# A second phase with three rounded matmul pairs and re-ordered engine queues

## The chip, the cores and the metric

The kernel runs on one core of one Trainium2 chip. The metric is the device time of one execution in microseconds. TensorE is PE (its weight loads PEld), VectorE is DVE, ScalarE is ACT, GpSimd is POOL, SyncE is SP.

## The reference

The input is 16 x 512 tokens of width 128 (8192 tokens). Cut to what matters:

```
xn = layernorm(x)
Q  = xn Wq + bq;  s = softmax(Q Q^T / sqrt(128)) Q            # per sequence of 512
logits = xn phi^T + phi_b                                     # 64 experts x 32 slots
D = softmax over a slot axis, C = softmax over the expert axis
X~ = D^T xn ; clip ; layernorm ; tanh ; Y~ = X~ expert_w + expert_b
x  = x + s * silu(C Y~)
xn = layernorm(x)
i, r = sigmoid gates of xn; a = exp(8 r log sigmoid(lam))
h_t = a_t h_(t-1) + sqrt(1 - a_t^2 + 1e-6) (i * xn W_in)      # scan over the sequence
s  = rmsnorm(h) W_out
g  = silu(sigmoid(xr W_r) * (relu(xk W_k)^2 W_v))             # xr, xk: mixes with the token before
out = x + s * g
```

All of it is float32. Products that need more than one rounded pass are made from a high part (rounded to fp32r) and a low part (what the rounding left).

## The kernel before, in words

The first phase (`tensor1`, `scalar1`, ...) goes over 128 units of 128 tokens by 1024 slots, writes the exponentials of the logits to HBM and accumulates X~. A short middle (`tensor1b`, ...) makes the expert outputs and holds them on chip as a high and a low part (`YHI`, `YLO`). The change touches only the second phase, `tensor2`, `scalar2`, `vector2`, `gpsimd2` and `sync2`, lines 1111 to 2347.

The second phase handles NB = 16 batches of 512 tokens. Each batch passes three stages in successive iterations of a software pipeline: the mixture output and the attention (batch i - 1 and i), then layernorm, gates and scan (i - 2), then the state norm, the output gate and the store (i - 3). The functions are the steps. The order in which each engine gets them is written out by hand, one list per engine inside `for i in range(-2, NB)` and then a tail list for the last batches. Engines run their list strictly in order and wait on semaphores; nothing else sets the order.

Per batch the mixture takes 16 chunks. A chunk is turned by four transposes (`exps_turned`, L1219), copied and rounded on ACT (`chunk_high`, L1585), its rest is formed on DVE (`chunk_low`, L1917), and `combine` adds three fp32r matmuls (L1229, L1230, L1232). `ct` has two banks, the chunk copies three. The attention steps are `project`, `values`, `scores`, `probabilities`, `scaled`, `turn`, `turn_high`, `turn_low` and `weigh`.

Seven matmuls per batch are in plain fp32, which the trace shows as two instructions each: `mean` (L1301, x minus its mean, by the matrix `CENTRE`), `variance` (L1309, mean of squares), `state_mean` (L1352), `ffn_k`, `ffn_r`, `ffn_v` and `state_out`.

ACT computes Exp, Ln, Tanh, Square, Copy, Identity and Relu. Its functions come from table sets, one loaded at a time. `log_table` (L1698) loads the set named `natural_log_exp_and_others`, `tanh_table` (L1702) the set named `exp_and_others`. Both are called by hand at places in the list:

```
def log_table(i):
    if i >= 0:
        e.preload_act_table_set("natural_log_exp_and_others")
```

In the loop each is called twice per iteration. The Ln steps are `state_log`, `deviation_log` and `input_log`; the Tanh steps are `ffn_tanh`, `decay_tanh`, `y_tanh`, `input_tanh` and `ffn_r_tanh`. The Tanh of the middle phase (L1041) has no such call in the code ahead of it; the only call before it, at L359, names the set with Ln. POOL multiplies the loaded exponentials by their weights (`weigh_exps`, L146), eight instructions per batch, and does three element-wise steps of a batch (L2275, L2280, L2286).

## Time and profile before

| quantity | value |
|---|---|
| median of 3 runs | 1187.49 us (1187.18 to 1188.07) |
| span of the profiled execution | 1184.2 us |
| PE, DVE, ACT, POOL busy in the span | 97%, 89%, 83%, 81% |
| granted TensorE clock, mean | 0.998 |

The page gives the profiled execution by its span, from its first to its last instruction; a run's time holds 3.3 us more at the median, which lies around the span. A busy time is the union of the engine's records. Records of one engine can overlap, since the next instruction starts before the last has drained, so the distance between two starts is often shorter than a record. The second phase begins near 600 us; its steady part repeats every 35 us.

### The profile page before, as it was taken

Reading aid. Unit: us, or ns where it says so; the run is one execution under the profiler, and the core shown is the slowest. Engines: PE = TensorE matmul, PEld = TensorE weight load, DVE = VectorE, ACT = ScalarE, POOL = GpSimd, SP = SyncE. Lnnn points to the kernel's source line nnn. Section 1 sums busy time; section 2 is a strip of 40 time slices with the busy share of each in tenths; the row PEclk is TensorE's granted clock in tenths of the full one; section 3 lists DMA queues with packets and bytes.
Section 4 is the critical chain, followed back from the end, with each engine's and each line's share of the span. In section 5 each row is a group of like instructions: output and inputs, shape, how many; then the busy total and the mean of one; then the engine's idle time right before and its main releaser. Section 6 shows DMA issues by size and latency. Waiting matters only on the chain. (4 is left out here: it accounts for less than half of the span.)

```text
span 1184.2 us, 17639 instructions
## 1 busy us (share of the span) xinstructions
PE 1144.7 (97%) x5097; PEld 787.9 (67%) x5097; DVE 1050.1 (89%) x1608; ACT 981.7 (83%) x2128; POOL 958.9 (81%) x770
## 2 busy tenths in 40 slices
PE   5999999999999999999989999999999999999996
PEld 3666666565666666666457777777777777777764
DVE  7999999999999999999767888888888888888887
ACT  5877877877766766766668999999999999999998
POOL 3998999898999999999788777878777788877751
PEclk9999999999999999999999999999999999999999
DMA  4445435434424432443754444344444444444420
GB/s 131 152 152 200 141 140 182 153 128 164 155 109 160 155 133 113 161 156 129 225 188 154 131 142 143 119 147 128 142 143 143 131 128 134 141 128 142 142 72 18
DMA packets 125263, 167.36 MB, mean 141 GB/s; under 512 B 7536, under 2 KB 102000, under 8 KB 125040
## 3 DMA queue, kind: packets, MB, share of 16 engines
q1 hardware_dynamic: 123984, 165.71, 41.4%
q8 instruction: 42, 0.69, 0.2%
q10 hardware_dynamic: 1184, 0.53, 0.2%
q14 instruction: 53, 0.43, 0.1%
HBM read 90.71 MB, written 75.50 MB: 140 GB/s over the span
## 5 line engine op out<-in xcount | busy, mean ns | idle before, releaser
L146 POOL TENSOR_TENSOR exp_slots_loaded<-exp_slots_loaded,slot_max 128x1024 f32<-128x1024 f32 x128 | 323.2, 2545 | 6.6 <-DMA exp_slots_loaded<-exp_slots 3.2
L858 POOL TENSOR_TENSOR dd<-ed,rz 128x512 f32<-128x512 f32 x256 | 267.6, 1051 | 24.7 <-ACT rz L688 23.4
L563 PE MATMUL acc<-dd,xns 128*128 128x512 f32 x512 | 261.1, 592 | 0.7 <-POOL dd L858 0.7
L1917 DVE TENSOR_TENSOR clo<-ct,chi 128x512 fp32r<-128x512 f32 x256 | 171.5, 681 | 24.3 <-ACT chi L1585 21.6
L176 POOL TENSOR_TENSOR ch<-exp_slots_loaded 128x512 f32<-128x512 f32 x128 | 165.9, 1296 | 32.0 <-ACT exp_slots_loaded L666 30.9
L795 DVE TENSOR_REDUCE mr<-lg 128x16 fp32r<-128x512 f32 x256 | 168.0, 685 | 19.3 <-PE lg L506 16.9
L657 ACT ACTIVATE ed<-lg 128x512 f32<-128x512 f32 x256 | 145.6, 594 | 40.3 <-PE lg L540 38.4
L666 ACT ACTIVATE exp_slots_loaded<-lg 128x512 f32<-128x512 f32 x256 | 145.5, 594 | 26.4 <-PE lg L549 24.4
L1585 ACT ACTIVATE chi<-ct 128x512 fp32r<-128x512 f32 x256 | 147.7, 597 | 11.8 <-PE ct L1219 8.3
L1219 PE MATMUL ct<-identity,exp_slots_loaded 128*128 128x128 f32 x1024 | 150.9, 273 | 5.6 <-POOL exp_slots_loaded L146 3.1
L811 DVE TENSOR_REDUCE zd<-ed 128x32 f32<-128x1024 f32 x128 | 154.6, 1208 | 1.5 <-ACT ed L657 1.5
L804 DVE TENSOR_REDUCE mr<-lg 128x32 fp32r<-128x1024 f32 x128 | 155.5, 1215 | 0.0
L1219 PEld LDWEIGHTS ct<-identity,exp_slots_loaded 128*128 128x128 f32 x1024 | 124.0, 140 | 35.5 <-POOL exp_slots_loaded L146 8.4
L549 PE MATMUL lg<-shift_experts_to_slots,mt 128*128 128x512 f32 x256 | 144.9, 596 | 0.7 <-ACT ed L657 0.7
L504 PE MATMUL lg<-phi_then_expert_out,xn_transposed 128*128 128x512 f32 x256 | 140.7, 550 | 0.5 <-ACT exp_slots_loaded L666 0.3
L1229 PE MATMUL yac<-chi,phi_then_expert_out 128*128 128x512 f32 x256 | 128.5, 502 | 0.0
L563 PEld LDWEIGHTS acc<-dd,xns 128*128 128x128 f32 x512 | 95.6, 192 | 22.1 <-issue 2.9
L1232 PE MATMUL yac<-clo,phi_then_expert_out 128*128 128x512 f32 x256 | 102.4, 400 | 0.9 <-DVE clo L1917 0.9
L506 PE MATMUL lg<-phi_then_expert_out,xn_transposed 128*128 128x512 f32 x256 | 102.3, 399 | 0.0
L505 PE MATMUL lg<-phi_then_expert_out,xn_transposed 128*128 128x512 f32 x256 | 101.7, 397 | 0.0
L1230 PE MATMUL yac<-chi,phi_then_expert_out 128*128 128x512 f32 x256 | 101.5, 396 | 0.0
L549 PEld LDWEIGHTS lg<-shift_experts_to_slots,mt 128*128 128x128 f32 x256 | 48.2, 188 | 77.4 <-ACT ed L657 62.0
(315 smaller groups left out, 2500.2 us busy)
## 6 DMA issues: line engine op xcount, KB each, us to landing
exp_slots<-exp_slots_loaded SPq DMA_DIRECT2D x128, 512.0 KB, 3.4
exp_slots_loaded<-exp_slots SPq DMA_DIRECT2D x128, 512.0 KB, 3.5
xns<-xn_rows SPq DMA_DIRECT2D x128, 64.0 KB, 1.9
b_xraw<-in_xT SPq DMA_DIRECT2D x16, 256.0 KB, 3.8
out_t<-b_ti SPq DMA_DIRECT2D x15, 256.0 KB, 2.1
expert_w_late<-in_expert_w SPq DMA_DIRECT2D x5, 512.0 KB, 11.1
xn_rows<-slot_sum SPq DMA_DIRECT2D x8, 256.0 KB, 2.5
expert_w_early<-in_expert_w SPq DMA_DIRECT2D x3, 512.0 KB, 5.8
```

Of the source, the lines that this page charges most:

```text
L146: e.tensor_tensor(rows, rows, joined(SM, b)[:, h].unsqueeze(2).broadcast_to([P, TPB, GC * EPC, NP]), ALU.mult).then_inc(s_we)
L176: e.tensor_tensor(ch[v % 2][:, :], ec[v % RE][:, 0:BANK], ec[v % RE][:, BANK:HS], ALU.add).then_inc(s_ch)
L549: e.matmul(lg[v % 2][:, bank(k)], mt[v % 2][:, :], S2M[:, bank(k)], start=False, stop=True, skip_group_check=True).then_inc(s_s2)
L563: e.matmul(acc[k][:, :], xns[v % RX][:, :], dd[v % RX][:, bank(k)], start=tile == 0, stop=tile == NT - 1, skip_group_check=True).then_inc( ...
L657: e.activation(ed[v % RD][:, bank(k)], lg[v % 2][:, bank(k)], ACT.Exp).then_inc(s_ed)
L795: e.tensor_reduce(mr[v % 2][:, k * HN // 2:(k + 1) * HN // 2], lg[v % 2][:, bank(k)].rearrange("q (n p) -> q n p", p=NP), AX_X, ALU.max).t ...
L804: e.tensor_reduce(mr[v % 2][:, HN:G], lg[v % 2][:, :].rearrange("q (n p) -> q p n", p=NP), AX_X, ALU.max).then_inc(s_mx)
L811: e.tensor_reduce(zd[v % 2][:, :], ed[v % RD][:, :].rearrange("q (n p) -> q n p", p=NP), AX_X, ALU.add).then_inc(s_zd)
L858: e.tensor_tensor(dd[v % RX][:, bank(k)].rearrange("q (n p) -> q n p", p=NP), ed[v % RD][:, bank(k)].rearrange("q (n p) -> q n p", p=NP), ...
L1219: done = e.transpose(ct[c % 2][:, rows(k)], ECL[:, g // GC % RL, k, c % GC * P:(c % GC + 1) * P], IDENT[:, :])
L1585: e.activation(chi[g % RC][:, :], ct[c % 2][:, :], ACT.Copy).then_inc(c_h)
L1917: e.tensor_tensor(clo[g % RC][:, :], ct[c % 2][:, :], hi_f32(chi[g % RC][:, :]), ALU.subtract).then_inc(c_l)
```

## The change

`mean`, `variance` and `state_mean` no longer multiply fp32 data. Each of their inputs is rounded to a high part on DVE (`first_high`, `squares_high`, `state_high`), POOL forms the low part (`first_low`, `squares_low`, `state_low`), and PE makes two fp32r matmuls (`two`). The parts are put into the no longer used tiles of `XT` (`tiles_of(i + 1, ...)`). `state_mean` writes to `lp[2]` except for batch 14, and `state_out` then waits for `state_log`. `scaled`, `scaled_r` and `scaled_k` use Copy with a scale column in place of Identity with a scale and a bias column. In the loop, `log_table` and `tanh_table` are called once per iteration each. The lists of all engines are re-ordered, loop and tail; in SP's list one load is moved behind the load of x. The order of ACT is shown whole, since the prediction follows it; those of PE, DVE, POOL and SP are left out. PE's new order for the part that the prediction walks through is: `exps_turned(4)`, `scores(0)`, `scores(1)`, `input_product(i - 3)`, `combine(2)`, `exps_turned(5)`, `combine(3)`, `scores(2)`, `ffn_r(i - 3)`. POOL's new list has the three low parts between its multiplications: `first_low(i)` after multiplication 3, `state_low(i - 1)` after 5, `squares_low(i)` after 6.

```diff
-            CENTRE = WRAW[:, 0, :]
+            CENTRE_R, MEAN_R = XT[:, 0, 0, :], XT[:, 1, 0, :]
+            CENTRE = hi_f32(CENTRE_R)
...
+            def by_tile(T):
+                return T[:, :].rearrange("q (n d) -> q n d", d=TILE)
+
+            def two(e, out, w, i, parts):
+                e.wait_ge(S[parts], 2 * i + 1)
+                e.matmul(out, w, tiles_of(i + 1, 0), start=True, stop=False)
+                e.wait_ge(S[parts], 2 * i + 2)
+                return e.matmul(out, w, tiles_of(i + 1, 1), start=False, stop=True)
 
 
             LAST = NB - 1
...
 
                 def mean(i):
                     if within(i):
-                        e.wait_ge(S["res"], i + 1)
                         if i:
                             e.wait_ge(S["f1"], i)
                         else:
-                            e.wait_ge(s_zero, 2)
-                        e.matmul(lp[0][:, :], CENTRE, B[f"x1{i % 2}"][:, :], start=True, stop=True).then_inc(S["mn"])
+                            e.wait_ge(s_zero, 3)
+                        two(e, lp[0][:, :], CENTRE_R, i, "x1_parts").then_inc(S["mn"])
 
                 def variance(i):
                     if within(i):
-                        e.wait_ge(S["sq"], i + 1)
                         if i:
                             e.wait_ge(S["ix"], i)
-                            e.wait_ge(S["hl"], i)
-                        e.matmul(lp[1][:, :], MEAN[:, :], B["ty"][:, :], start=True, stop=True).then_inc(S["vr"])
+                        two(e, lp[1][:, :], MEAN_R, i, "sq_parts").then_inc(S["vr"])
 
                 def decay_gate(i):
                     if within(i):
...
-                        e.matmul(lp[1][:, :], MEAN[:, :], B["a2"][:, :], start=True, stop=True).then_inc(S["hm"])
+                        if i == LAST - 1:
+                            e.wait_ge(S["ix"], i + 1)
+                        else:
+                            e.wait_ge(S["kr"], i + 1)
+                        two(e, state_bank(i)[:, :], MEAN_R, i, "hq_parts").then_inc(S["hm"])
 
                 def state_out(i):
                     if within(i):
-                        e.wait_ge(S["hh"], i + 1)
-                        e.wait_ge(S["kr"], i + 1)
+                        e.wait_ge(S["hl"], i + 1)
                         if i == LAST - 1:
                             e.wait_ge(S["ix"], nth(1))
                         e.matmul(lp[2][:, :], WRAW[:, W_OUT, :], B["hh"][:, :], start=True, stop=True).then_inc(S["po"])
...
-                        e.activation(B[f"e{r}"][:, :], B[f"e{r}"][:, :], ACT.Identity, bias=one(EPS, 3),
+                        e.activation(B[f"e{r}"][:, :], B[f"e{r}"][:, :], ACT.Copy,
                                      scale=one(nmx, 4 * r + 3)).then_inc(A["p"])
 
...
-                        e.activation(B["aa"][:, :], lp[1][:, :], ACT.Ln, bias=one(EPS, 1)).then_inc(S["hl"])
+                        e.activation(B["aa"][:, :], state_bank(i)[:, :], ACT.Ln, bias=one(EPS, 1)).then_inc(S["hl"])
 
                 def state_inverse(i):
...
@@ -1769,145 +1781,145 @@
                 for i in range(-2, NB):
                     chunk_high(i - 1, 4)
+                    input_log(i - 3)
+                    input_root(i - 3)
                     next_factors(i)
                     probabilities(i - 1, 0)
                     chunk_high(i - 1, 5)
+                    probabilities(i - 1, 1)
+                    scaled(i - 1, 0)
                     ffn_r_tanh(i - 3)
-                    probabilities(i - 1, 1)
                     chunk_high(i - 1, 6)
-                    scaled(i - 1, 0)
-                    state_squares(i - 3)
-                    scaled(i - 1, 1)
                     probabilities(i - 1, 2)
                     chunk_high(i - 1, 7)
+                    state_squares(i - 3)
+                    log_table(i - 1)
+                    scaled(i - 1, 1)
+                    chunk_high(i - 1, 8)
                     scaled(i - 1, 2)
-                    chunk_high(i - 1, 8)
-                    ffn_tanh(i - 3)
-                    log_table(i - 1)
-                    state_log(i - 3)
+                    squares(i - 2)
                     chunk_high(i - 1, 9)
                     probabilities(i - 1, 3)
                     chunk_high(i - 1, 10)
                     scaled(i - 1, 3)
-                    squares(i - 2)
-                    state_inverse(i - 3)
+                    state_log(i - 3)
                     chunk_high(i - 1, 11)
                     turn_high(i - 1, 0)
                     chunk_high(i - 1, 12)
+                    state_inverse(i - 3)
                     deviation_log(i - 2)
-                    tanh_table(i - 1)
                     deviation_inverse(i - 2)
+                    ffn_tanh(i - 3)
                     turn_high(i - 1, 1)
                     chunk_high(i - 1, 13)
+                    scaled_k(i - 2)
+                    scaled_r(i - 2)
                     chunk_high(i - 1, 14)
-                    scaled_k(i - 2)
                     turn_high(i - 1, 2)
-                    scaled_r(i - 2)
+                    decay_tanh(i - 2)
+                    tanh_table(i - 1)
                     chunk_high(i - 1, 15)
+                    turn_high(i - 1, 3)
+                    decay(i - 2)
                     chunk_high(i, 0)
-                    decay_tanh(i - 2)
-                    decay(i - 2)
-                    turn_high(i - 1, 3)
+                    y_tanh(i - 1)
                     decay_squares(i - 2)
+                    attended(i - 1)
                     chunk_high(i, 1)
-                    y_tanh(i - 1)
-                    log_table(i - 1)
-                    attended(i - 1)
-                    input_log(i - 2)
-                    tanh_table(i - 1)
+                    ffn_k_relu(i - 2)
                     query(i)
                     chunk_high(i, 2)
                     chunk_high(i, 3)
+                    value_high(i)
+                    ffn_k_squares(i - 2)
                     input_tanh(i - 2)
-                    ffn_k_relu(i - 2)
-                    value_high(i)
-                    input_root(i - 2)
-                    ffn_k_squares(i - 2)
             
 
+                tanh_table(LAST)
                 chunk_high(LAST, 4)
+                input_log(LAST - 2)
                 probabilities(LAST, 0)
                 chunk_high(LAST, 5)
+                input_root(LAST - 2)
+                scaled(LAST, 0)
+                probabilities(LAST, 1)
+                probabilities(LAST, 2)
                 ffn_r_tanh(LAST - 2)
-                probabilities(LAST, 1)
                 chunk_high(LAST, 6)
-                scaled(LAST, 0)
-                state_squares(LAST - 2)
                 scaled(LAST, 1)
-                probabilities(LAST, 2)
                 chunk_high(LAST, 7)
                 scaled(LAST, 2)
+                ffn_tanh(LAST - 2)
+                state_squares(LAST - 2)
                 chunk_high(LAST, 8)
-                ffn_tanh(LAST - 2)
-                log_table(LAST)
+                probabilities(LAST, 3)
+                chunk_high(LAST, 9)
+                squares(LAST - 1)
+                scaled(LAST, 3)
+                chunk_high(LAST, 10)
                 state_log(LAST - 2)
-                chunk_high(LAST, 9)
-                probabilities(LAST, 3)
-                chunk_high(LAST, 10)
-                scaled(LAST, 3)
-                squares(LAST - 1)
-                state_inverse(LAST - 2)
                 chunk_high(LAST, 11)
                 turn_high(LAST, 0)
+                state_inverse(LAST - 2)
                 chunk_high(LAST, 12)
+                chunk_high(LAST, 13)
                 deviation_log(LAST - 1)
-                tanh_table(LAST)
                 deviation_inverse(LAST - 1)
+                log_table(LAST)
                 turn_high(LAST, 1)
-                chunk_high(LAST, 13)
-                chunk_high(LAST, 14)
+                log_table(LAST)
                 scaled_k(LAST - 1)
                 turn_high(LAST, 2)
-                scaled_r(LAST - 1)
+                chunk_high(LAST, 14)
                 chunk_high(LAST, 15)
                 decay_tanh(LAST - 1)
+                turn_high(LAST, 3)
                 decay(LAST - 1)
-                turn_high(LAST, 3)
+                y_tanh(LAST)
+                scaled_r(LAST - 1)
+                log_table(LAST)
                 decay_squares(LAST - 1)
-                y_tanh(LAST)
-                log_table(LAST)
-                ffn_k_relu(LAST - 1)
+                input_tanh(LAST - 1)
                 last_squares(0)
+                last_squares(1)
                 input_log(LAST - 1)
                 last_deviation_log(0)
-                last_squares(1)
                 last_deviation_inverse(0)
+                last_deviation_log(1)
+                ffn_k_relu(LAST - 1)
                 input_root(LAST - 1)
-                last_deviation_log(1)
                 last_deviation_inverse(1)
-                tanh_table(LAST)
-                input_tanh(LAST - 1)
+                ffn_r_tanh(LAST - 1)
+                ffn_k_squares(LAST - 1)
                 last_decay_tanh(0)
+                log_table(LAST)
+                last_decay(0)
+                state_squares(LAST - 1)
+                last_decay_squares(0)
+                ffn_tanh(LAST - 1)
                 last_input_tanh(0)
-                ffn_k_squares(LAST - 1)
-                last_decay(0)
                 last_decay_tanh(1)
-                ffn_r_tanh(LAST - 1)
-                last_ffn_r_tanh(0)
+                last_input_tanh(1)
                 last_decay(1)
-                last_decay_squares(0)
-                last_decay_squares(1)
-                last_input_tanh(1)
-                state_squares(LAST - 1)
-                log_table(LAST)
                 last_input_log(0)
                 state_log(LAST - 1)
+                last_decay_squares(1)
+                last_input_root(0)
+                last_ffn_r_tanh(0)
+                state_inverse(LAST - 1)
                 last_input_log(1)
-                last_input_root(0)
-                tanh_table(LAST)
                 last_input_root(1)
-                state_inverse(LAST - 1)
+                last_ffn_tanh(0)
+                last_state_squares(0)
+                last_state_log(0)
                 last_ffn_r_tanh(1)
-                ffn_tanh(LAST - 1)
-                last_state_squares(0)
-                last_ffn_tanh(0)
+                last_state_inverse(0)
+                last_state_squares(1)
                 last_ffn_tanh(1)
-                log_table(LAST)
-                last_state_squares(1)
-                last_state_log(0)
-                last_state_inverse(0)
                 last_state_log(1)
                 last_state_inverse(1)
+                tanh_table(LAST)
+                tanh_table(LAST)
 
             def vector2(e):
...
+
+                def constants(i):
+                    if i == 0:
+                        e.wait_ge(S["q_p"], 1)
+                        e.tensor_tensor(CENTRE_R, IDENT[:, :], MEAN[:, :], ALU.subtract).then_inc(s_zero)
+                        e.tensor_copy(MEAN_R, MEAN[:, :]).then_inc(s_zero)
+
+                def first_high(i):
+                    if within(i):
+                        e.wait_ge(S["res"], i + 1)
+                        e.wait_ge(S["q_p"], i + 2)
+                        e.tensor_copy(tiles_of(i + 1, 0), by_tile(B[f"x1{i % 2}"])).then_inc(S["x1_parts"])
+
+                def squares_high(i):
+                    if within(i):
+                        e.wait_ge(S["sq"], i + 1)
+                        e.tensor_copy(tiles_of(i + 1, 0), by_tile(B["ty"])).then_inc(S["sq_parts"])
+
+                def state_high(i):
+                    if within(i):
+                        e.wait_ge(S["hq"], i + 1)
+                        e.tensor_copy(tiles_of(i + 1, 0), by_tile(B["a2"])).then_inc(S["hq_parts"])
 
                 def normalise(i):
                     if within(i):
```

## Rows read from the trace of the kernel before

**Rows 1.** The page: busy tenths of the span in 40 slices, PE and its granted clock.

```profile
PE   5999999999999999999989999999999999999996
...
PEclk9999999999999999999999999999999999999999
```

**Rows 2.** Stretches of 35 us in the steady part: busy us of PE, PEld, DVE, ACT, POOL; clock.

```profile
892.00:927.00 35.00, 35.00 (x184) 26.77 (x183) 30.12 (x52) 34.16 (x60) 27.50 (x16) 1.00 0.43 138
962.01:997.00 34.99, 34.99 (x184) 26.74 (x183) 30.06 (x52) 34.13 (x59) 27.45 (x16) 1.00 0.43 136
```

**Rows 3.** PE in order of time: start us, us, instruction, count.

```profile
964.03 0.60 PE L1219 MATMUL ct<-identity,exp_slots_loaded 128*128 128x128 f32 x4
964.46 1.02 PE L1301 MATMUL lp<-b_x,weights 128*128 128x512 f32 x2
965.32 1.02 PE L1360 MATMUL lp<-b_hh,weights 128*128 128x512 f32 x2
...
982.29 0.39 PE L1235 MATMUL at<-xn_transposed,weights_high 128*128 128x512 f32 x1
982.52 0.40 PE L1236 MATMUL at<-xn_transposed,weights_high 128*128 128x512 f32 x1
982.76 0.39 PE L1237 MATMUL at<-xn_transposed,weights_low 128*128 128x512 f32 x1
982.99 0.40 PE L1229 MATMUL yac<-chi,phi_then_expert_out 128*128 128x512 f32 x1
```

**Rows 4.** Groups of the second phase: count, busy us, mean ns of one, idle before.

```profile
L1569 ACT ACTIVATE b_e<-b_e,epsilons,nmx 128x512 f32<-128x512 f32 x64 | 51.7, 811 | 0.5 <-DVE nmx L1938 0.5
L1670 ACT ACTIVATE b_a<-b_a,epsilons 128x512 f32<-128x512 f32 x15 | 10.7, 713 | 0.0
L1974 DVE CAST r_xh<-xn 128x512 fp32r<-128x512 f32 x15 | 6.3, 418 | 0.0
L2280 POOL TENSOR_TENSOR r_xl<-xn,r_xh 128x512 fp32r<-128x512 f32 x15 | 19.3, 1290 | 60.8 <-DVE r_xh L1974 60.8
```

**Rows 5.** ACT in order of time, in a steady batch.

```profile
979.28 0.60 ACT L1577 ACTIVATE b_ty<-yac 128x512 f32<-128x512 f32 x1
979.90 1.28 ACT L1698 ACT_TABLE_LOAD   x1
981.19 0.60 ACT L1564 ACTIVATE b_st<-at 128x512 f32<-128x512 f32 x1
981.69 0.71 ACT L1670 ACTIVATE b_a<-b_a,epsilons 128x512 f32<-128x512 f32 x1
982.42 1.28 ACT L1702 ACT_TABLE_LOAD   x1
```

**Rows 6.** ACT in order of time, in the first batch, where no Ln runs yet.

```profile
633.90 1.28 ACT L1698 ACT_TABLE_LOAD   x1
635.20 0.60 ACT L1564 ACTIVATE b_st<-at 128x512 f32<-128x512 f32 x1
635.82 1.28 ACT L1702 ACT_TABLE_LOAD   x1
```

**Rows 7.** Table loads, whole span, by line; count and ns (minimum, median, maximum), first and last start.

```profile
L1698 ACT ACT_TABLE_LOAD  x34: 1283/1283/1283, 619.5 to 1176.4; - x34
L1702 ACT ACT_TABLE_LOAD  x33: 1283/1283/1283, 624.8 to 1172.4; - x33
L1041 ACT ACT_TABLE_LOAD  x1: 1283/1283/1283, 591.9 to 591.9; - x1
```

**Rows 8.** Waits of POOL between 752 and 1032 us: total, times, longest.

```profile
POOL r_xl L2280 <- DVE r_xh L1974: 31.0, 8, 3.9
POOL b_ty L2286 <- DVE b_ty L1953: 19.4, 8, 2.4
POOL r_ql L2275 <- DVE r_qh L1924: 9.1, 8, 1.1
```

**Rows 9.** The tail list, stretch as in rows 2.

```profile
1127.93:1184.20 56.27, 45.02 (x198) 30.35 (x196) 45.00 (x85) 47.75 (x88) 15.68 (x10) 0.96 0.12 38
```

**Rows 10.** ACT's last instruction.

```profile
1180.03 0.42 ACT L1768 ACTIVATE b_e<-b_e 128x256 f32<-128x256 f32 x1
```

More of the change, by code:

```diff
@@ L1439, in tensor2 @@
+                    weigh(i - 2, 3)
                     exps_turned(i - 1, 1)
-                    combine(i - 2, 14)
-                    combine(i - 2, 15)
-                    weigh(i - 2, 2)
-                    weigh(i - 2, 3)
+                    ffn_k(i - 3)
+                    project(i - 1)
                     exps_turned(i - 1, 2)
-                    input_gate(i - 3)
-                    input_product(i - 3)
-                    project(i - 1)
                     combine(i - 1, 0)
@@ L1625, in scaled_r @@
                             e.wait_ge(S["f2"], i)
-                        e.activation(B["xr"][:, :], x_in, ACT.Identity, bias=one(EPS, 3), scale=one(VEC, V_MUR)).then_inc(S["mr"])
+                        e.activation(B["xr"][:, :], x_in, ACT.Copy, scale=one(VEC, V_MUR)).then_inc(S["mr"])
                 def scaled_k(i):
@@ L1632, in scaled_k @@
                             e.wait_ge(S["pk"], i)
-                        e.activation(B["xk"][:, :], x_in, ACT.Identity, bias=one(EPS, 3), scale=one(VEC, V_MUK)).then_inc(S["mk"])
+                        e.activation(B["xk"][:, :], x_in, ACT.Copy, scale=one(VEC, V_MUK)).then_inc(S["mk"])
                 def input_tanh(i):
```

222 lines of the change are left out of this document (125 added, 97 removed), and 2 rows, old and new, of the table S.

## The prediction, made before the changed kernel ran

> **What bounds the kernel now.** I read the page's slices first: PE is busy in nine tenths or more of nearly every slice, at the full granted clock [rows 1]. A high share is an average, so I looked at the steady part of the second phase in stretches of its own period, 35.0 us: there PE has no gap at all, ACT is covered for 34.1, DVE for 30.1 and POOL for 27.5 [rows 2]. PE's records overlap, so I checked by starts that this is real work. Rounded matmuls start 0.23 to 0.24 us apart, a plain fp32 one takes 0.86 us to the next start, four transposes 0.43 [rows 3]. A batch has 48 + 12 + 12 + 3 + 9 = 84 rounded matmuls (combine, scores, weigh, project, three gates), 7 plain ones and 21 sets of four transposes: 84 x 0.233 + 7 x 0.86 + 21 x 0.435 = 34.7, which is the period within 1%. So PE sets the period, and ACT is right behind it. ACT's 0.87 us of gaps, with 0.1 of lost overlap at each of some five gaps (a 0.60 record lets the next start 0.50 later [rows 5]), leaves about 33.7 us of work per batch. DVE has 5 us to spare and POOL 7.5.
>
> The end is another matter. The tail list lasts 56.3 us, and ACT is covered for 47.75 of them, PE for 45.0 [rows 9]. ACT's last instruction ends at 1180.45 [rows 10], 3.75 before the end. ACT leads the tail.
>
> **The change, part by part.**
>
> *PE.* Three plain matmuls of 0.86 become pairs of 0.47: 3 x 0.39 = 1.17 us less per batch, 33.8 in place of 35.0. The old time is on the path.
>
> *DVE.* Three casts of 0.42 each [rows 4], +1.3: 31.4. *POOL.* Three subtractions of 1.29, +3.9: 31.35. Both are covered by the period as long as their waits shrink (a rival, below). Of the new waits, PE's on a low part has nearly all of PE's queue behind it; the lists put other PE work between the step that makes the input and the pair, so I take these waits at zero, with 1 us per batch as the other end. The changed bank of `state_mean`, the move of SP's load and the setup on DVE I cost at nothing: one instruction, or work in the spare time of [rows 2].
>
> *ACT, Copy for Identity.* An SBUF operation with two column operands takes 0.811, with one 0.713 [rows 4]: 0.1 x 6 = 0.6 less per batch.
>
> *ACT, the table loads.* The calls are half as many, but the needs are not. In the new loop list the order is: `input_log` (Ln), `ffn_r_tanh` (Tanh), the call of the Ln set, `state_log` and `deviation_log` (Ln), `ffn_tanh`, `decay_tanh` (Tanh), the call of the Tanh set, `y_tanh`, `input_tanh` (Tanh), and around again to `input_log`. Ln and Tanh alternate twice per batch as before, and the calls no longer stand where the sets change: `input_log` runs with the Tanh set, `ffn_tanh` with the Ln set. The trace shows what then happens: the Tanh at L1041 comes with the Ln set loaded and no call ahead of it, and there is a load on its own line [rows 7]. So loads are placed where they are missing. It also shows that a called load is executed though nothing needs it: in the first batch both are, with only a copy between [rows 6], and the 34 + 33 loads are exactly the calls that the lists make.
>
> Which set a placed load takes for an Ln isn't shown. The code names the set that has Exp too, by hand and before its first Ln, which would be needless if it came by itself; so I take a set with Ln alone, and the Exp behind it needs another load. In the loop the count is the same either way, as the way back comes at `input_root` or at `ffn_r_tanh`. Going down the list: `input_log`, `input_root`, the call of the Ln set, `ffn_tanh`, and the call of the Tanh set, which is loaded already. Five per iteration, four before, from i = 3 on (13 iterations); iterations 1 and 2 have two and three. In the tail I count 26 ahead of the last `last_state_inverse`, where there were 7: it alternates at `input_log`, `state_log`, `deviation_log` of batch 14, at each of `last_input_log` and `last_state_log`, each time there and back.
>
> One load costs 1.29 to the next start, and the instruction ahead of it loses its overlap (0.62 in place of 0.50 to the next start [rows 5]): 1.41.
>
> The Trainium skill, ScalarE: Activation LUTs (What ACT_TABLE_LOAD costs), puts a switch at 2.66 us, 1.283 for the load and 1.38 for a drain. The load agrees to the nanosecond; the drain is not there, since the next instruction starts 1.29 after [rows 5]. By the page's figure the 19 further loads of the tail alone would be 51 us, an estimate, and the kernel would come out near 1245. I go by the row. The same page (Table sets) says that a compiler pass puts a load before every activation that needs one; L1041 agrees.
>
> **The sum.** Steady part: ACT 33.7 - 0.6 + 1.4 = 34.5 us of work, PE 33.8. Neither fits the other: at the head of the loop ACT now has load, Ln, load, Exp, `next_factors` and `probabilities(0)` between two chunks. From the start of `chunk_high(4)` to the end of `probabilities(0)` that is 0.5 + 1.4 + 0.7 + 1.4 + 0.5 + 0.3 + 0.7 = 5.5 us. PE has for it two `scores`, a product, two `combine` (5 x 0.70) and one set of transposes (0.44), 3.9 us, and then `scores(2)` waits for that probability: 1.5 us idle. With 0.4 more near `ffn_tanh`, where Exp, Ln, Exp, load and Tanh stand between two chunks (estimated, since PE can have three chunks ready): 33.8 + 1.5 + 0.4 = 35.7. The ends are 34.5 (all hidden) and 37 (both stalls in full, and waits on the low parts). So 13 x 0.7 = +9. The first iterations have PE's saving only in part: -1.
>
> Tail: work 47.75 + 19 x 1.41 + 1.25 (`input_log` and `input_root` of batch 13 come in from the loop) - 0.6 = 75.2; of the 4.8 us of gaps I keep 2 (ends 1 and 6); and 3.75 behind ACT: 81, where 56.3 was: +24.5.
>
> In all 1184.2 + 9 - 1 + 24.5 = 1217 by the span; runs lie 3.3 above it: 1220. With the ends of the steady part (-6.5 to +26) and of the gaps the likeliest case has 1204 to 1240. A difference under 0.2% can't be told from none.
>
> **The rivals.**
>
> *The repeated call costs nothing.* The compiler could drop a load of the set that is there already. The executed calls of [rows 6] were needless but did change the set, so they don't rule it out. Then 80 loads in place of 98: four per iteration, ACT at 33.1, period about 35.0 with the stall at the loop's head half closed, 22 in the tail less the idle kept: 1187.5 + 0 - 1 + 21 = 1207.
>
> *A placed load for Ln takes the set with Exp too.* Six fewer in the tail, 8.5 us: 1211. For it: a pass that looks ahead would. Against it: the name in the code.
>
> *POOL becomes the bound.* It waits 59.5 us in 8 batches for DVE, 7.4 per batch [rows 8]. 31.35 + 7.4 = 38.8, over the 35.7, if the waits keep their length; it decides from 4.4 us per batch of waits. +3.1 x 13 = +40: 1260. Against it: these waits are slack of a loop that PE paces, and the new list puts the subtractions between multiplications.
>
> *The relief of PE wins (other side).* Both of the first two rivals hold, the tail has 18 loads, 11 more than before, and its gaps take 4: +15.5 - 4 + 0.7 = +12. The new order hides the blocks so that PE stays the bound at 33.9: 13 x -1.1 = -14, and -1 at the start: 1184. The point from which it decides is a period below about 34.1. That the change does as it is called, two loads per batch in place of four and a tail with as few, would give 1187.5 - 15 x 1.17 = 1170; the order of Ln and Tanh in the list rules it out, unless one set held both, and then nothing would have been loaded in between before.
>
> **How the numbers follow.** Forecast 0.52, dropped repeats 0.15, other set 0.15, POOL 0.08, relief of PE 0.08, as it is called 0.02. Slower over 0.2% is the first four, 0.90; of the other 0.10 I give 0.07 to faster and 0.03 to the 0.2% around no change (1184 is near its edge). The range leaves out POOL as the bound and the lowest of the faster cases: 1197 to 1241.
>
> **What would show it.** Plain matmuls at the three lines gone, pairs 0.23 apart. Table loads on lines of Ln, Exp and Tanh steps: 98 in all in the second phase, 28 in the tail; 80 or 92 would be the rivals. ACT covered more than PE in a steady batch, and PE with a gap ahead of the third `scores`, released by ACT. A period of 35.7; 33.9 would show me wrong on the coupling, 38 would be POOL. A tail of 80 us led by ACT. I am wrong altogether if the loads are 30 to 40 in number.

## The result, and the profile after

The changed kernel takes 1296.46 us (median of 4 runs, 1295.71 to 1296.63), where the kernel before took 1187.51 on the same chip: 1.0917 times as long [1.0902, 1.0933]. The direction was forecast; the size (1220, at most 1241) was not. In the profiled execution the span is 1294.8 us, 110.6 more than before.

To see where they are, cut the span at the scan of a batch, an instruction that both kernels run once per batch. Thirteen periods, from the scan of the first batch to that of the fourteenth, last 1224.37 - 678.56 = 545.8 us, 41.7 to 42.5 each and 41.9 at the median; before it was 1130.58 - 675.89 = 454.7, or 35.0 each. So the start holds +2.7, the steady part +91.1, and what follows that scan +16.8 (70.4 for 53.6).

The stretches, columns as in [rows 2]: length, busy us of PE, PEld, DVE, ACT, POOL, clock, DMA share, GB/s. First two steady periods and the end of the kernel after:

```profile
847.01:889.12 42.11, 35.72 (x185) 26.38 (x183) 37.15 (x55) 35.31 (x61) 32.06 (x18) 1.00 0.35 113
930.86:973.07 42.21, 35.67 (x185) 26.40 (x184) 37.22 (x55) 35.31 (x61) 32.06 (x18) 1.00 0.34 113
1224.37:1294.80 70.43, 46.32 (x183) 33.34 (x181) 42.92 (x78) 65.83 (x97) 19.49 (x12) 0.82 0.07 23
```

and the end of the kernel before, cut at the same scan (the list of [rows 9] begins a little earlier):

```profile
1130.58:1184.20 53.62, 42.37 (x184) 28.44 (x182) 42.47 (x79) 45.38 (x83) 15.12 (x9) 0.96 0.12 39
```

The reader is to see two things. In the steady part no engine is covered for the whole period any more: the fullest is DVE with 37.2 of 42.2, and PE has 6.5 us of gaps where it had none. So the engines now wait for each other in turn. And ACT and POOL stand near their forecast (35.3 for 34.5, 32.06 for 31.35), while DVE stands at 37.2 where I had 31.4: its instructions take 5.8 us more than their durations before add up to.

Which of them, the groups of DVE in the second phase of the kernel after tell (line, op, tiles, shapes, count | busy us, mean ns | idle before):

```profile
L2054 DVE TENSOR_TENSOR_SCAN b_hh<-b_aa,vectors,b_ti 128x512 f32<-128x512 f32 x15 | 50.6, 3372 | 0.0
L2074 DVE TENSOR_TENSOR b_ti<-b_aa,b_x 128x512 f32<-128x512 f32 x15 | 37.4, 2490 | 0.5
L2029 DVE TENSOR_SCALAR b_a<-b_a 128x512 f32<-128x512 f32 x15 | 21.1, 1403 | 0.3 <-ACT b_a L1631 0.3
L1989 DVE CAST xn_transposed<-b_ty 128x512 fp32r<-128x512 f32 x15 | 19.8, 1317 | 0.0
L1984 DVE CAST xn_transposed<-b_x 128x512 fp32r<-128x512 f32 x15 | 9.3, 622 | 0.0
L1994 DVE CAST xn_transposed<-b_a 128x512 fp32r<-128x512 f32 x15 | 6.2, 412 | 0.0
```

The kernel before, the same three steps in the same view:

```profile
L2020 DVE TENSOR_TENSOR_SCAN b_hh<-b_aa,vectors,b_ti 128x512 f32<-128x512 f32 x15 | 22.6, 1505 | 0.0
L2040 DVE TENSOR_TENSOR b_ti<-b_aa,b_x 128x512 f32<-128x512 f32 x15 | 10.4, 692 | 0.5
L1995 DVE TENSOR_SCALAR b_a<-b_a 128x512 f32<-128x512 f32 x15 | 6.2, 411 | 0.0
```

The same instruction with the same operands takes 3.37 us in place of 1.50 (the scan), 2.49 in place of 0.69 (`output`), 1.40 in place of 0.41 (`one_minus`). These three alone are 1.87 + 1.80 + 0.99 = 4.7 us per batch, and the cast of the squares adds 0.9. What stands beside the scan and `output` is POOL's multiplication of the exponentials; beside `one_minus` it is another POOL instruction, the product at L2341. The timelines of DVE and POOL (start us, us, instruction, count, [idle before <-releaser]) around one of each, kernel after:

```profile
930.13 0.69 DVE L2046 SCALAR_TENSOR_TENSOR b_ti<-b_ti,b_a 128x512 f32<-128x512 f32 x1
930.86 3.52 DVE L2054 TENSOR_TENSOR_SCAN b_hh<-b_aa,vectors,b_ti 128x512 f32<-128x512 f32 x1
...
930.90 5.63 POOL L146 TENSOR_TENSOR exp_slots_loaded<-exp_slots_loaded,slot_max 128x1024 f32<-128x1024 f32 x2 [2.02 <-DVE b_ti L2046]
...
949.72 2.77 DVE L2074 TENSOR_TENSOR b_ti<-b_aa,b_x 128x512 f32<-128x512 f32 x1
...
949.16 5.57 POOL L146 TENSOR_TENSOR exp_slots_loaded<-exp_slots_loaded,slot_max 128x1024 f32<-128x1024 f32 x2
...
959.75 1.50 DVE L2029 TENSOR_SCALAR b_a<-b_a 128x512 f32<-128x512 f32 x1
...
959.63 1.33 POOL L2341 TENSOR_TENSOR b_ty<-b_ty,b_st 128x512 f32<-128x512 f32 x1
```

and around the scan of the kernel before:

```profile
990.67 1.37 DVE L2020 TENSOR_TENSOR_SCAN b_hh<-b_aa,vectors,b_ti 128x512 f32<-128x512 f32 x1
...
990.06 0.89 POOL L130 TENSOR_TENSOR slot_joined<-slot_sum 128x128 f32<-128x128 f32 x1
990.92 8.01 POOL L146 TENSOR_TENSOR exp_slots_loaded<-exp_slots_loaded,slot_max 128x1024 f32<-128x1024 f32 x3
```

Before, POOL was still at a small step when the scan began, and its multiplication came 0.25 us later. After, POOL has been idle for 2.02 us and is released by the very instruction (L2046, `scan_input`) that also feeds the scan; both start within 0.04 us, and the scan takes 2.1 us longer, about one multiplication. `output` begins 0.56 behind the start of a multiplication and takes 2.1 longer too. `one_minus` begins 0.12 behind POOL's product and takes 1.1 longer, so about 1 us of the 5.8 is not the multiplications'.

Who pays for it shows in the waits of ACT over six steady batches of the kernel after (engine, line, waited for: us in total, times, longest), with PE's behind them:

```profile
ACT b_aa L1619 <- DVE b_ti L2074: 12.9, 6, 2.1
ACT b_a L1692 <- DVE b_hh L2054: 11.9, 6, 2.0
ACT chi L1597 <- PE ct L1232: 11.4, 18, 1.7
...
PE yac L1245 <- DVE clo L1929: 12.3, 12, 1.5
PE at L1278 <- ACT b_e L1561: 9.4, 6, 1.6
```

ACT's two longest waits are for exactly these two instructions: `decay_tanh` needs `output`, `state_squares` needs the scan, 4.1 us per batch together. The chunks behind them on ACT come late, and DVE's low parts, and PE. No wait in the lists of PE, DVE and ACT for these six batches ends on POOL: nobody waits for what POOL makes.

The second suspect, the loads, came as forecast. In order of time on ACT, kernel after:

```profile
964.88 0.60 ACT L1597 ACTIVATE chi<-ct 128x512 fp32r<-128x512 f32 x1
965.49 1.28 ACT L1682 ACT_TABLE_LOAD   x1
966.79 0.72 ACT L1682 ACTIVATE b_a<-b_a,epsilons 128x512 f32<-128x512 f32 x1
967.53 1.28 ACT L1687 ACT_TABLE_LOAD   x1
968.82 0.63 ACT L1687 ACTIVATE b_a<-b_a 128x512 f32<-128x512 f32 x1
```

and in the groups of the whole span:

```profile
L1710 ACT ACT_TABLE_LOAD x19 | 24.4, 1283 | 0.3
L1714 ACT ACT_TABLE_LOAD x17 | 21.8, 1283 | 0.3
L1682 ACT ACT_TABLE_LOAD x15 | 19.2, 1283 | 0.3
L1687 ACT ACT_TABLE_LOAD x14 | 18.0, 1283 | 0.2
L1677 ACT ACT_TABLE_LOAD x14 | 18.0, 1283 | 0.3
```

With 18 more on fourteen lines of Ln, Exp and Tanh steps that is 97 in the second phase (67 before, [rows 7]), five in each steady batch. The Ln at L1682 got a set without Exp, and the Exp at L1687 another load. L1710 and L1714 are the calls: all 19 of the Ln set, and 17 of the 18 of the Tanh set. Repeated calls are executed (L1710 at 1243.41 and, with one copy between, at 1245.32; L1714 in every batch). Of the last two calls in the list, with nothing between them, only one has a record; no run tells why.

### The profile page after: what moved, and what is told of

Same layout as the page of the kernel before. It is cut to its first block, busy times and chain, and to the rows that moved or that the text cites. A ratio compares the mean times of both kernels' runs of the same rounds, so it can differ in the third digit from the quotient of the medians.

```text
span 1294.8 us, 17761 instructions
## 1 busy us (share of the span) xinstructions
PE 1159.8 (90%) x5097; PEld 788.4 (61%) x5097; DVE 1150.5 (89%) x1654; ACT 1017.9 (79%) x2158; POOL 1028.3 (79%) x815
## 4 chain that ended last, share of the span: by engine, by line
DVE 19%; ACT 17%; PE 10%; issue 8%; ACTq 0%; DVEq 0%
DVE clo L1929 4%; DVE b_hh L2054 4%; PE ct L1232 3%; ACT chi L1597 3%; DVE b_ti L2074 3%; PE yac L1245 2%; ACT L1710 2%; ACT L1682 1%; DVE b_a L2029 1%; DVE xn_transposed L1989 1%; DVE b_f L2040 1%; ACT L1677 1%; PE yac L1242 1%; PE yac L1243 1%; ACT b_e L1581 1%
## 5 line engine op out<-in xcount | busy, mean ns | idle before, releaser
L146 POOL TENSOR_TENSOR exp_slots_loaded<-exp_slots_loaded,slot_max 128x1024 f32<-128x1024 f32 x128 | 332.6, 2610 | 66.5 <-DMA exp_slots_loaded<-exp_slots 32.6
L176 POOL TENSOR_TENSOR ch<-exp_slots_loaded 128x512 f32<-128x512 f32 x128 | 165.7, 1295 | 31.4 <-ACT exp_slots_loaded L666 30.3
L795 DVE TENSOR_REDUCE mr<-lg 128x16 fp32r<-128x512 f32 x256 | 168.0, 685 | 18.9 <-PE lg L506 16.5
L1597 ACT ACTIVATE chi<-ct 128x512 fp32r<-128x512 f32 x256 | 152.1, 595 | 35.7 <-PE ct L1232 34.5
L1245 PE MATMUL yac<-clo,phi_then_expert_out 128*128 128x512 f32 x256 | 105.2, 411 | 26.6 <-DVE clo L1929 26.6
L1242 PE MATMUL yac<-chi,phi_then_expert_out 128*128 128x512 f32 x256 | 115.4, 451 | 0.1
L1243 PE MATMUL yac<-chi,phi_then_expert_out 128*128 128x512 f32 x256 | 101.4, 396 | 0.0
```

Of the source, the lines that this page charges most:

```text
L146: e.tensor_tensor(rows, rows, joined(SM, b)[:, h].unsqueeze(2).broadcast_to([P, TPB, GC * EPC, NP]), ALU.mult).then_inc(s_we)
L176: e.tensor_tensor(ch[v % 2][:, :], ec[v % RE][:, 0:BANK], ec[v % RE][:, BANK:HS], ALU.add).then_inc(s_ch)
L795: e.tensor_reduce(mr[v % 2][:, k * HN // 2:(k + 1) * HN // 2], lg[v % 2][:, bank(k)].rearrange("q (n p) -> q n p", p=NP), AX_X, ALU.max).t ...
L1597: e.activation(chi[g % RC][:, :], ct[c % 2][:, :], ACT.Copy).then_inc(c_h)
```

## The experiments

Theory A, held: DVE's instructions are held back by POOL's multiplications, which the new lists put in front of them. Theory B: it is the five loads per batch that stretch the period, by more than I had, and DVE's long records are a by-product. Theory C: POOL has too much work with the three low parts, or PE waits for them.

**e1: the loads taken away.** `Ln` becomes `Square`, so the logarithms are left out, and no call is made; the trace then has no load in the second phase.

```diff
-  e.activation(..., ACT.Ln, ...)
+  e.activation(..., ACT.Square, ...)
-  e.preload_act_table_set(...)      # log_table, tanh_table
+  pass
```

> The changed kernel with no table loads in the second phase: the three Ln steps compute Square (same operands, so the state norm, the deviation and the input factor are wrong) and both calls are left out. Theory A (the DVE instructions held behind POOL pace the loop, 41.9 us): ACT has 7 us less per batch but the scan, the output step and the casts stay long; period 38 to 41, median 1240 to 1280. Theory B (the five loads pace it): period 34 to 35.5, median 1170 to 1190.

Measured: 1221.30 us, 1.0295 [1.0265, 1.0325]. The period is 38.1, the scan still takes 3366 ns on average. The end, from the scan of the fourteenth batch on, is 47.2 us, where it was 70.4. So taking the loads away gives 75 us: 3.8 per batch (about 50), 23 in the end, the rest at the start. The period is in the range that A expected, the time below it, since the end gave back so much. Not all of the 3.8 is the loads' own time: `output` falls from 2490 to 1058 ns as POOL's work now meets DVE's elsewhere, while the cast of the squares rises from 1317 to 1841. Without a single load the new kernel is still 2.95% slower than before: B can't be all.

**e2: the low parts taken away.** The second matmul of each pair takes whatever lies in the low tiles, and PE doesn't wait for it, so the low parts are left out; POOL has 3.9 us less per batch.

```diff
-  first_low(i) ... state_low(i - 1) ... squares_low(i)    # POOL
-  e.wait_ge(S[parts], 2 * i + 2)                          # PE
```

> The changed kernel without POOL's three low parts; both rounded matmuls are still made, the second from what lies in the low tiles (its sum is wrong). The casts stay. Theory A: POOL has 3.9 us less per batch, but its multiplications still start just ahead of the scan and the output step, so the scan stays near 3.5 and the period falls by 1 to 3 us: 1250 to 1280. Theory C (PE's waits on low parts pace it): period 36 or less, under 1215.

Measured: 1313.30 us, 1.107 [1.103, 1.1111]. Less work, and slower than the change by 17 us. That ends C, and missed what I expected. The groups of DVE in e2 show what came with it:

```profile
L2053 DVE TENSOR_TENSOR_SCAN b_hh<-b_aa,vectors,b_ti 128x512 f32<-128x512 f32 x15 | 50.6, 3371 | 0.0
L2073 DVE TENSOR_TENSOR b_ti<-b_aa,b_x 128x512 f32<-128x512 f32 x14 | 36.6, 2617 | 0.5
L1993 DVE CAST xn_transposed<-b_a 128x512 fp32r<-128x512 f32 x15 | 31.7, 2115 | 0.2 <-ACT b_a L1691 0.2
```

The multiplications begin at other moments, and the cast of the state's squares, 412 ns in the change, is held for 1.7 us as well.

**e3: POOL released by the scan itself**, not by its input, so that the scan is first.

```diff
-  e.wait_ge(S["gt"], i - 1)     # weigh_exps, k == 4
+  e.wait_ge(S["hh"], i - 1)
```

> The changed kernel, in which POOL's multiplication 4 waits for the scan instead of for the scan's input. Theory A: the scan falls from 3.5 to about 1.4 us, ACT's 2.0 us wait for it is gone; POOL starts 1.4 later. Period down by 1 to 2.5 us, 1260 to 1280. If the long scan were not caused by POOL's start: no shorter scan, same or slower than 1296.

Measured: 1292.09 us, 1.0892 [1.086, 1.0923]. Groups of DVE in e3:

```profile
L2074 DVE TENSOR_TENSOR b_ti<-b_aa,b_x 128x512 f32<-128x512 f32 x15 | 37.4, 2493 | 0.5
L1994 DVE CAST xn_transposed<-b_a 128x512 fp32r<-128x512 f32 x15 | 35.5, 2365 | 0.0
L1989 DVE CAST xn_transposed<-b_ty 128x512 fp32r<-128x512 f32 x15 | 27.6, 1843 | 0.0
L2054 DVE TENSOR_TENSOR_SCAN b_hh<-b_aa,vectors,b_ti 128x512 f32<-128x512 f32 x15 | 19.4, 1293 | 0.0
```

The order of release does decide who is held: the scan is at 1293 ns now. But the 2.1 us moved on to the next cast (412 to 2365), and the time gained is 4 us of 109, where 16 or more were expected; the intervals of e3 and of the change overlap. One hold taken away isn't a hold less.

**e4: the new orders without the split.** The three plain matmuls stay as before, no casts, no low parts; lists, calls and `Copy` as in the change.

```diff
-  two(e, lp[0][:, :], CENTRE_R, i, "x1_parts")
+  e.matmul(lp[0][:, :], CENTRE, B[f"x1{i % 2}"][:, :], start=True, stop=True)
```

> The new orders, Copy and calls with the three matmuls in plain fp32 as before: no casts, no low parts. PE has 1.17 us more per batch, DVE 3 casts less, POOL 3 subtractions less. If the orders and loads are what costs: period 37.5 to 41, 1235 to 1285. If the split into parts is what costs: near 35 to 36, 1190 to 1215.

Measured: 1300.26 us, 1.096 [1.0929, 1.0992]: the whole loss, and 4 us more, is there without the split, and more than I expected of the orders. The scan (3372 ns) and `output` (2488) are as long as in the change. The lists and the calls lose the time. If the split itself gives anything back, it is those 4 us, and the intervals of e4 and of the change touch.

**e5 and e6: the multiplications halved**, with the loads of the change (e5) and without any (e6). Only the first two of four blocks of `weigh_exps` are multiplied.

```diff
-  e.tensor_tensor(rows, rows, ..., ALU.mult)
+  e.tensor_tensor(rows[:, 0:2], rows[:, 0:2], ..., ALU.mult)
```

> The changed kernel in which POOL's multiplications of exponentials do two of their four tiles (half the elements; the rest of the weighting is left out). Loads as in the changed kernel. Theory A (DVE held behind POOL's instructions): the longest hold falls from 2.1 us to 1 us, the scan to 2 to 2.5 us, DVE's busy time by 3 us; period from 41.9 to 38.5 to 40. Theory B (the loads alone): DVE's times fall but the period stays over 41.

> Both at once: half of the multiplications and no table loads (Ln steps as Square). If loads and holds explain the excess between them, the period comes to PE's own 33.8 to 34.8, from 38.1 without loads alone; median 1150 to 1175. If a third cause is there (waits between PE and the new orders), it stays over 36.

Measured: e5 1243.68 us, 1.0484 [1.0463, 1.0505], with the scan at 2353 ns and `output` at 1534; e6 1177.55 us, 0.9927 [0.9907, 0.9947]. The periods of the four, from scan to scan, at the median:

```
                        five loads   no loads
multiplications whole      41.9        38.1
multiplications half       38.2        35.1
```

A stretch of one period of e6, columns as above:

```profile
847.00:882.12 35.12, 34.57 (x184) 26.68 (x183) 32.44 (x55) 28.80 (x56) 22.93 (x18) 1.00 0.42 134
```

The period of e5 is just under what A expected, that of e6 and its time are just over their ranges. Both causes are real, of equal size, and nearly add up: the loads give 3.8 or 3.1, half of the multiplications 3.7 or 3.0. With both gone PE is covered again for 34.57 of 35.12 us. Half sized multiplications also take 9 us per batch of work off POOL, so e5 alone would not tell a hold from a full POOL; e2 does that, where POOL had 3.9 us less and nothing was gained, and so does the list of waits above, in which nobody waits for POOL.

**e7: a load only where the set changes**, and for every Ln the set that has Exp too.

```diff
-  e.preload_act_table_set(...)        # log_table, tanh_table
+  with_log()    # ahead of each Ln: loads its set unless it is there
+  with_tanh()   # ahead of each Tanh, the same
```

> The changed kernel in its own order, but each load placed where the needed set changes, for Ln always the set that has Exp too: 4 per batch in place of 5, and 17 or so in the tail in place of 26. Outputs complete. By loads at 0.76 us of period each (3.8 us for five): 41.1 in the steady part, -11; tail about 9 loads less, -10; 1273 to 1280.

Measured: 1279.96 us, 1.079 [1.0768, 1.0812], with 67 loads again in the second phase, as many as before, and as expected. The period is 41.3, the end 62.9. So calls in the right places would have saved 16.5 us of 109: 0.7 per batch on average (the fifth load) and 7.5 in the end. By e1 the other four loads are worth 3.8 - 0.7 = 3.1 per batch in this order, where [rows 2] had four inside PE's time.

**e8: the split in the old order.** The lists and calls of the kernel before; the mean and the mean of the state's squares in two passes, their casts and low parts set into the old lists; `state_mean` stands two steps later in PE's.

```diff
     value_low(i)            # DVE
+    first_high(i - 1)
...
     chunk_low(i, 6)
+    state_high(i - 2)
```

> The kernel before with its own orders and loads, and two of the three matmuls (mean and state mean) in two rounded passes, the casts and low parts put into the old lists. PE has 0.78 us less per batch. If PE still paces it: 15 x 0.78 = 12 less, 1175. If the two casts (0.8) and two low parts (2.6) are held or hold the scan: between 1180 and 1205.

Measured: 1225.19 us, 1.0319 [1.0302, 1.0336], period 37.4, over both ranges expected. Here the scan is as before (1504), but the new cast `first_high` (L1981) takes 1955 ns, and ACT's exponentials wait 1.6 us per batch for a maximum behind it on DVE (`b_e` L1558 for `nmx` L1942: 8.0, 5 times). So the split meets holds in the old list too. How much of the 2.4 us of period they make isn't shown.

**e9: the hold by itself.** Thirteen equal instructions on DVE, 128 x 512; behind the fifth, POOL is released for four multiplications of 128 x 1024; once for each of four forms.

```
DVE: out = a + b      (both SBUF)      POOL: big = big * factor, four
DVE: out = ps + b     (PSUM and SBUF)        times, from DVE's fifth
DVE: cast a to the rounded type
DVE: scan over a, b
```

> A kernel by itself, none of the reference's work: DVE runs 13 times each of four forms on 128x512 (sum of two SBUF tiles, sum of a PSUM and an SBUF tile, cast of an SBUF tile to fp32r, scan of two SBUF tiles), and POOL four multiplications of 128x1024 beside the last eight. Theory A (held by the operands): the first, third and fourth form get longer by up to a POOL instruction (2.1 us) or make POOL longer; the PSUM form stays at 0.68. If any DVE instruction is slowed by POOL, the PSUM form grows too; if none is, the long ones in the changed kernel have another cause.

Each form's line (count: minimum/median/maximum ns, first and last start), then the groups with their means:

```profile
L72 DVE TENSOR_TENSOR from_two_sbuf<-left,right x13: 679/685/2828, 6.8 to 22.7; 128x512 f32<-128x512 f32 x13
L74 DVE TENSOR_TENSOR from_psum_and_sbuf<-ps,right x13: 677/677/680, 23.3 to 30.4; 128x512 f32<-128x512 f32 x13
L76 DVE CAST from_cast<-left x13: 414/421/2564, 36.1 to 48.7; 128x512 fp32r<-128x512 f32 x13
L77 DVE TENSOR_TENSOR_SCAN from_scan<-left,right x13: 1252/1252/3293, 49.0 to 71.3; 128x512 f32<-128x512 f32 x13
L95 POOL TENSOR_TENSOR multiplied<-multiplied,factor x16: 2337/2550/3229, 10.1 to 64.8; 128x1024 f32<-128x1024 f32 x16
...
L77 DVE TENSOR_TENSOR_SCAN from_scan<-left,right 128x512 f32<-128x512 f32 x13 | 23.5, 1881 | 0.0
L72 DVE TENSOR_TENSOR from_two_sbuf<-left,right 128x512 f32<-128x512 f32 x13 | 16.5, 1342 | 0.0
L76 DVE CAST from_cast<-left 128x512 fp32r<-128x512 f32 x13 | 13.0, 1077 | 4.9 <-POOL multiplied L95 4.9
L74 DVE TENSOR_TENSOR from_psum_and_sbuf<-ps,right 128x512 f32<-128x512 f32 x13 | 7.9, 677 | 0.0
```

Mean less median, times 13, over four multiplications: an addition of two SBUF operands loses 13 x 0.657 / 4 = 2.1 us to each multiplication, the cast 2.1, the scan 2.0, and the addition with one PSUM operand nothing (its longest is 680 ns). That is nearly the multiplication's own 2.34. And it falls on one instruction for each multiplication: four of the thirteen additions take 2.82 to 2.83 us, the other nine 0.68 to 0.69. So it is no sharing of bandwidth, which would stretch each by some share: an instruction of a held form waits the multiplication out. This carries A for the scan, `output` and the casts; the form of `one_minus`, one SBUF operand and a scalar, isn't among the four, and its hold is read from the trace of the change alone.

The Trainium skill, SBUF — State Buffer (SBUF: two separate sides), says it in a rule: the port pair shared by DVE and GpSimd is "an exclusive lock, not a bandwidth split", and a DVE instruction in a two-port mode, or with two SBUF inputs against a GpSimd one that reads SBUF, blocks or is blocked for the whole instruction. The four forms agree: three held, the one with a PSUM operand not. That the cast is held would be its two-port mode by the page; the run shows only that it is.

**e10: the cast where POOL waits.** As e8, with `first_high` right behind `residual`, where POOL sits idle.

```diff
     residual(i - 1)         # DVE
+    first_high(i - 1)
     project_split(i)
...
-    first_high(i - 1)
```

> As the two splits in the old order, but the cast of x goes right behind the residual, where POOL waits for the query. Theory A: the cast falls from 1.96 to 0.42 us, ACT's wait of 1.6 us for the row maximum goes, and the period falls from 37.4 to 34.5 to 35.8: 1178 to 1200. If the added work itself is the cause, it stays at 1215 to 1225.

Measured: 1219.51 us, 1.0275 [1.0261, 1.0289]; I had expected 1178 to 1200. The cast is free (427 ns), and two others are held in its place: `scan_input` 692 to 1475, the state's cast 509 to 873. Period 37.25 for 37.38, and DVE is covered for 32.97 us of it, for 32.91 in e8. e3 again: the hold moves.

**e11: one split, its high part on ACT.** The old lists, `Copy` for `Identity`, only the mean in two passes, the high part made by ACT where DVE made it.

```diff
+    first_high(i - 1)       # ACT: e.activation(..., ACT.Copy)
...
+    first_low(i)            # POOL
```

> The kernel before with Copy for Identity, and only the mean in two rounded passes: high part by a Copy on ACT, low part on POOL behind multiplication 3. PE has 0.39 us less per batch, ACT 0.1 less, DVE nothing more. If nothing is held: 15 x 0.39 = 6 less, 1181. If POOL's 1.3 us more holds DVE as in the other splits: 1188 to 1200.

Measured: 1189.08 us, 1.0018 [1.0009, 1.0027]. No new instruction on DVE, and PE's 0.39 per batch is won on paper; but POOL's times move, `b_f` (L2029) is held to 2016 ns, from 1327, and the period is 35.1 on average, from 34.5 to 35.8.

**e12: the kernel before without its loads**, as a measure of what they cost there.

```diff
-  e.activation(..., ACT.Ln, ...)
+  e.activation(..., ACT.Square, ...)
-  e.preload_act_table_set(...)
```

> The kernel before without table loads in the second phase (Ln steps as Square). If a load costs only where nothing hides it: period stays 35.0, as PE has no gap, and the tail gives back 4 to 7 us of its seven loads; 1179 to 1183. If each costs 0.76 us of period as in the changed kernel: 45 us less.

Measured: 1194.83 us, 1.0069 [1.0051, 1.0087]: 67 loads fewer, and slower, where I had expected 1179 to 1183. Its groups of DVE:

```profile
L2020 DVE TENSOR_TENSOR_SCAN b_hh<-b_aa,vectors,b_ti 128x512 f32<-128x512 f32 x15 | 37.6, 2508 | 0.0
L2006 DVE SCALAR_TENSOR_TENSOR b_f<-b_xr,b_kr 128x512 f32<-128x512 f32 x15 | 29.3, 1953 | 0.0
```

The periods alternate between 36.7, with the scan at 3.5 us and `b_f` at 2.6, and 34.8, with both as before (1.37 and 1.3). So where nothing more is held, the four loads were worth 0.2 us: in the kernel before they were under PE's time. In the other batches, without the loads, more of DVE is held. The end, from the scan of the fourteenth batch on, is 1192.3 - 1140.3 = 52.0, for 53.6 with its 7 loads.

Of the kernels that leave nothing out, none is faster than the kernel before.

## Why the prediction was right and wrong

*Loads: right.* 98 forecast by going down the list, 97 found; the one missing is the second of the two calls that end the list. Five in a steady batch; the repeated call executed, a set without Exp for a placed Ln, 1.29 us to the next start. All 26 that I counted ahead of the last `last_state_inverse` are there. Both rivals on the loads are out.

*PE and ACT at the head of the loop: right.* PE's wait for the probability at the third `scores` was forecast at 1.5 us; it is 9.4 / 6 = 1.6, released by ACT, and in e1, without the loads, it is left once, with 0.7 us. `Copy` came out at 719 ns where I had 713. That PE would not wait for a low part held too.

*The end: right, mechanism and size.* The forecast counts from the first chunk of the tail list, so the measurement has to as well. The stretches from there, after and before:

```profile
1216.63:1294.80 78.17, 51.89 (x201) 36.77 (x199) 49.01 (x90) 73.39 (x108) 21.52 (x14) 0.82 0.08 27
1127.82:1184.20 56.38, 45.13 (x198) 30.46 (x197) 45.11 (x85) 47.86 (x88) 15.79 (x10) 0.96 0.12 38
```

That is +21.8 for +24.5, with ACT covered for 73.4 of 78.2 us. The scan stands later in the new tail, 7.7 us behind that chunk in place of 2.8, which is why the cut at the scan gave +16.8 only. By the cut at the first chunk the start is 2.7 us shorter (forecast 1), and the thirteen iterations between are 91.6 longer (forecast 9). e1 puts 23.2 us of the end on the loads. Without any load the tail takes 55.0 us in the new order (e1) and 54.8 in the old (e12), so the new order of the end by itself is neither better nor worse. One thing has no term in the forecast: the granted clock of TensorE in the tail is 0.82, with stretches at 1.2 GHz, for 0.96 before and 0.98 in e1; PE is covered for only 51.9 of the 78.2 us. No run separates what that costs.

*The failed step: DVE.* "Three casts of 0.42 each, +1.3: 31.4. ... Both are covered by the period as long as their waits shrink." The period is no sum of durations taken from the old order. DVE's were true only beside the POOL instructions that stood there, and 5.8 us of holds came on top: 37.2. Of these, as means of the groups, 4.7 are on the scan, `output` and `one_minus`, 0.9 on the cast of the squares. Taking half of POOL's multiplication work away gives 3.7 us of the period back, 48 us over the 13. That is the larger part of the 82 by which the steady part was missed (91 for 9). No rival had this mechanism either.

*A second term was too small: the loads in the steady part.* I had the fifth load and the coupling at 35.7 - 33.8 = 1.9 us per batch; e5 against e6 gives 3.1, e1 against the change 3.8, part of it by holds that move with the loads (`output` in e1). The cover [rows 2] for the four old loads was a list that put other work of ACT ahead of time, and the new list has less of it: I summed the instructions of the new list, and followed its waits at one place only. This reason is argued; the numbers are run.

In steps, per batch: 33.8 forecast for PE alone, 35.1 measured with neither cause (e6), 38.2 with the loads (e5), 41.9 with both; against 35.7 that is 1.3 + 1.2 + 3.7, and 6.2 x 13 = 81.

*The rivals.* POOL as the bound gave 38.8 for the period and 1260, nearer than my forecast, but by another mechanism: POOL's busy time is 32.06 of 42.1, and e2 shows that less of it doesn't help. The relief of PE, 1.17 us per batch or 17.6 in all, is covered by everything else: e4, without it, is 4 us slower. The change as it is called was out from the trace of before, as argued.

*What stays open.* Why e6 is at 35.1 and not 33.8: its scan still takes 2.4 us, so some holds are left, but no run separates them from other waits. How the 3.8 and the 3.7 divide what is common to both (3.1 + 3.0 + 0.7). What SP's moved load does: in the six batches POOL waits 13.9 us for the loads of the exponentials, which sets when its multiplications begin, where the kernel before has 0.6 us of such waits in thirteen; the move was not run by itself. And a list that keeps the casts clear of POOL wasn't found: e3 and e10 each freed one instruction and had another held, and in e11, with no cast on DVE, `b_f` was held longer.

## What to carry to other kernels

Before pricing an instruction of DVE from another order, look at what POOL runs beside it: a form with two SBUF operands, a cast or a scan can cost its own time plus the rest of POOL's instruction (2.1 us on 0.68, 0.42 or 1.25 in e9), and the addition with one PSUM operand did not. If POOL is released by the step that also feeds the next one on DVE, ask which starts first, and what comes next on DVE when that one is freed. And where function tables are called by hand, walk the list with the set in mind: a call that isn't at the change of set is executed in full and saves none.

## What the runs showed of the hardware

- A POOL multiplication of 128 x 1024 costs DVE 2.0 to 2.1 us if DVE has a held form to run, and nothing if it has not (e9); POOL's own goes up as well, from 2.34 to as much as 3.23 us.
- An instruction's record covers the hold: a scan of 1252 ns is shown with 3293 in e9 and 3.52 us in the kernel after, with no wait beside it. In the groups it looks like a slower instruction, in the chain of waits like DVE's work.
- With 3.9 us less work per batch on POOL the kernel got 17 us slower (e2 against the change), with 67 loads fewer 0.7% slower (e12 against before): what moves the meetings of the two engines can outweigh what it saves.
- A table load called for the set that is already there takes 1283 ns like any other (L1710 at 1245.32, behind the same call at 1243.41, kernel after).
